# Decoder layer: self attention's sums passed inside the chip, products by pairs of key blocks, feed-forward weights made in cross attention

## The reference

```python
x = x + self_attention(layernorm(x))     # causal; scores (q W_cross) k mixed with a shifted k by a gate
x = x + cross_attention(layernorm(x))    # 77 context tokens, a mask
x = x + ffn(layernorm(x))                # silu(x Wg) * (x Wu), then Wd; the weights are int32 / 127
# attention, per head:
attn = softmax(scores); out = attn @ v; y = concat(out) @ Wo
```

## Time and profile before

| | us |
|---|---|
| median of 3 runs (1131.58 to 1135.62) | 1133.68 |
| the profiled execution | 1134.03 |
| its span, first to last instruction | 1132.3 |
| TensorE busy | 1044.6 (92%) |
| VectorE busy | 748.3 (66%) |
| ScalarE busy | 571.1 (50%) |
| GpSimd busy | 224.3 (20%) |
| bytes moved | 113.66 MB, mean 100 GB/s |

### The profile page before, as it was taken

The page is one execution under the profiler, slowest core; times in us unless marked ns, Lnnn a source line. Parts: engine busy times, 40 slices in busy tenths (PEclk is TensorE's granted clock), DMA queues, the critical chain, the costliest instruction groups (busy, mean ns, idle before and its releaser), DMA issues. The chain is left out here.

```text
span 1132.3 us, 19037 instructions
## 1 busy us (share of the span) xinstructions
PE 1044.6 (92%) x7092; PEld 608.6 (54%) x7092; DVE 748.3 (66%) x1603; ACT 571.1 (50%) x1043; POOL 224.3 (20%) x191
## 2 busy tenths in 40 slices
PE   2888989999999999999999895689989899999997
PEld 2777434444444444444444463344444688888886
DVE  5999887777887887877786374356544555555552
ACT  1445147667776677677666664646646211111110
POOL 6545550000000000000000032600000133333331
PEclk9999779999999999999999996889989899999998
DMA  7259844333334444444020045848774211111101
GB/s 244 104 198 251 248 86 74 73 75 70 71 70 89 90 86 88 89 89 86 23 76 27 35 130 187 204 89 171 169 177 126 80 43 49 51 53 50 48 9 37
DMA packets 89811, 113.66 MB, mean 100 GB/s; under 512 B 13822, under 2 KB 74922, under 8 KB 88183
## 3 DMA queue, kind: packets, MB, share of 16 engines
q1 hardware_dynamic: 86071, 107.43, 38.3%
q10 hardware_dynamic: 3648, 5.02, 2.1%
HBM read 66.26 MB, written 45.45 MB: 99 GB/s over the span
## 5 line engine op out<-in xcount | busy, mean ns | idle before, releaser
L782 ACT ACTIVATE prob<-bank 128x512 f32<-128x512 f32 (+1 forms) x608 | 329.2, 575 | 180.2 <-PE bank L826 101.5
L734 DVE TENSOR_REDUCE pm<-bank 128x1 f32<-128x512 f32 (+3 forms) x608 | 364.3, 655 | 82.5 <-PE bank L810 62.0
L805 PE MATMUL bank<-stk,stq 96*128 96x512 bf16 (+3 forms) x768 | 226.6, 339 | 2.7 <-DVE pm L734 2.1
L822 PE MATMUL bank<-stq,stk 98*128 98x512 bf16 (+3 forms) x768 | 222.4, 328 | 0.9 <-ACT prob L782 0.8
L836 PE MATMUL bank<-prob,va 128*17 128x512 f32 (+3 forms) x1536 | 164.0, 500 | 0.0
L805 PEld LDWEIGHTS bank<-stk,stq 96*128 96x128 bf16 x768 | 70.1, 98 | 153.5 <-DVE pm L734 114.1
L1554 ACT ACTIVATE e_sg<-bank 128x512 f32<-128x512 f32 x48 | 28.7, 598 | 188.7 <-PE bank L135 188.7
L967 POOL TENSOR_TENSOR c_rstd<-c_ve,mhalf 128x4 f32<-128x4 f32 x8 | 8.1, 1010 | 521.3 <-DVE c_ve L128 521.3
L1311 ACT ACTIVATE xprob<-bank 80x512 f32<-80x512 f32 x128 | 72.3, 592 | 65.5 <-PE bank L1349 64.0
L822 PEld LDWEIGHTS bank<-stq,stk 98*128 98x128 bf16 x768 | 69.2, 98 | 56.7 <-issue 12.2
L810 PE MATMUL bank<-tri_q,identb 128*128 128x128 bf16 (+2 forms) x352 | 88.3, 251 | 0.0
(11 more groups left out here) (172 smaller groups left out, 1379.4 us busy)
## 6 DMA issues: line engine op xcount, KB each, us to landing
qk<-a_parts SPq DMA_DIRECT2D x32, 384.0 KB, 4.3
od<-u_out SPq DMA_DIRECT2D x16, 512.0 KB, 3.2
oin<-od SPq DMA_DIRECT2D x32, 256.0 KB
od<-xu SPq DMA_DIRECT2D x16, 512.0 KB, 3.9
xq<-c_parts SPq DMA_DIRECT2D x16, 384.0 KB, 2.9
xstq<-xq SPq DMA_DIRECT2D x32, 192.0 KB, 4.3
stq<-qk SPq DMA_DIRECT2D x28, 192.0 KB, 4.6
stk<-qk SPq DMA_DIRECT2D x14, 384.0 KB, 7.1
```

Of the source, the lines that this page charges most:

```text
L734: nc.vector.tensor_reduce(pm[:, k, h0:h0 + hb, r], src[:, 0:hb * w].rearrange("p (h w) -> p h w", h=hb), AX, ALU.max).then_inc(s_mxe, 1)
L782: nc.scalar.activation(prob[:, U % NPS, 0:hb * n], bank[STB[U % NSB]][:, 0:hb * n], ACT.Exp).then_inc(s_ex, 1)
L805: mm = nc.tensor.matmul(dst[:, h * w:(h + 1) * w], stq[i][0:R, half, h0 + h, r * P:(r + 1) * P], stk[i][0:R, h0 + h, k0:k0 + w], start=(h ...
L822: mm = nc.tensor.matmul(dst[:, h * n:(h + 1) * n], stk[i][0:RM, h0 + h, kt * P:(kt + 1) * P], stq[i][0:RM, half, h0 + h, q0:q0 + n], start ...
```

## The change

- The sums and the denominators of self attention go by DMA from `u_out` straight to on-chip tensors `oall` and `den`: eight DMAs a group in place of one store, and no loads of them later. `shares` waits for these DMAs; `quotients` works in place and waits for no load.
- Two sets of products are issued one after the other when the second one's scores are 3 units old; `NPS` is 16. Self attention has three sets of buffers in place of four.
- In the middle stage `load_later`, without the weights, and the last sequence's shares come first on SyncE, and the shares first on VectorE. The weights' making leaves the stage.
- The weights are loaded in groups 0, 1 and 6 of cross attention and made in twelve pieces of 384 columns: ScalarE's two instructions after unit 6's exponential in groups 1 to 12, GpSimd's one ahead of its other work there.

```diff
-        NPS, LAG, LATE = 12, 3, 3
+        joint_end = [sets[s - s % 2 + 1][3] for s in range(len(sets))]
+        NPS, LAG, LATE = 16, 3, 3
...
-            plan += [("p", s, -1) for s, x in enumerate(sets) if x[3] - 1 == NST + u - LAG]
-            plan += [("p", s, 0) for s, x in enumerate(sets) if x[3] - 1 == u - LAG]
+            plan += [("p", s, -1) for s in range(len(sets)) if joint_end[s] - 1 == NST + u - LAG]
+            plan += [("p", s, 0) for s in range(len(sets)) if joint_end[s] - 1 == u - LAG]
...
             def store(g):
+                b, i = g // GB, g % GB
                 sp.wait_ge(s_u, 2 * g + 2)
-                sp.dma_start(od[g:g + 1].rearrange("a h w r t -> (a h w r) t"), u_out[:, g % 2]).then_inc(us[g % 2], 16)
+                for h in range(HG):
+                    row = HD * (HG * (i % 2) + h)
+                    sp.dma_start(oall[row:row + HD, b, i // 2],
+                                 u_out[h * VW:h * VW + HD, g % 2]).then_inc(us[g % 2], 16)
+                    row = S // DT * (HG * i + h)
+                    sp.dma_start(den[row:row + S // DT, b],
+                                 u_out[h * VW + HD:h * VW + VC, g % 2]
+                                 .rearrange("a (c t) -> a c t", t=DT)).then_inc(us[g % 2], 16)
...
-                    if g + GB - 1 < G:
+                    if g + NB - 1 < G:
                         sp.wait_ge(s_pv, g * NST)
-                        load_self(sp, g + GB - 1)
+                        load_self(sp, g + NB - 1)
...
         def quotients(v, c, k):
-            v.wait_ge(ldo[c % 3], 32 * (c // 3 + 1))
+            b, u = c // 2, c % 2
             v.wait_ge(s_bc, KT * c + k + 1)
-            nc.vector.tensor_tensor(oin[:, c % 3, k], bank[EB if c < N_EARLY else BB[k]][:], oin[:, c % 3, k],
-                                    ALU.mult).then_inc(s_on, 1)
+            o = oall[:, b, k, u * CH:(u + 1) * CH]
+            nc.vector.tensor_tensor(o, bank[EB if c < N_EARLY else BB[k]][:], o, ALU.mult).then_inc(s_on, 1)
...
         def mid_sync(sp):
-            for w in range(2):
-                sp.wait_ge(us[w], 16 * (G // 2))
-            load_den(sp, B - 1)
-            load_outputs(sp, 3)
-            load_outputs(sp, 4)
+            load_later(sp)
+            store_shares(sp, B - 1)
+            load_shares(sp, B - 1)
             for c in range(NCH):
-                if c + 5 < NCH:
-                    load_outputs(sp, c + 5)
                 for n in range(KT):
                     store_queries(c, n)
-                if c == 0:
-                    store_shares(sp, B - 1)
-                    load_shares(sp, B - 1)
-                    load_later(sp)
-                if c == 4:
-                    load_last_weight(sp)
...
         def mid_vector(v):
+            shares(v, B - 1)
             for k in range(KT):
                 quotients(v, 3, k)
             sums2(v, 2)
             for c in range(NCH):
                 for n in range(KT):
                     split(c, n)
-                if c == 0:
-                    shares(v, B - 1)
...
+        def load_weight(sp, n):
+            if n == 2:
+                sp.wait_ge(s_fl, NPC)
+            src = (gate_t, up_t, down_t)[n]
+            sp.dma_start(iw[:, n % 2].rearrange("p (t n) -> p t n", n=src.shape[1]),
+                         src.rearrange("(t p) n -> p t n", p=P)).then_inc(s_iw[n], 16)
+
+        def ffn_weight_high(a, x):
+            n, j = x // NPC, x % NPC
+            a.wait_ge(s_iw[n], 16)
+            i = iw[:, n % 2, j * PW:(j + 1) * PW]
+            nc.scalar.activation(i.bitcast(F32), i, ACT.Identity, scale=WSCALE).then_inc(s_ff, 1)
+            a.wait_ge(s_ff, 2 * x + 1)
+            nc.scalar.activation(piece((wg, wu, wd)[n][:, 0], j), i.bitcast(F32), ACT.Identity).then_inc(s_ff, 1)
...
+                if g < 2:
+                    load_weight(sp, g)
+                if g == 6:
+                    load_weight(sp, 2)
...
         def cross_gpsimd(g):
+            for x in range(3 * NPC):
+                ffn_weight_low(g, x)
             for c in range(2):
                 quotients3(g, c)
...
+                    if u == NST2 - 2 and 1 <= g <= 3 * NPC:
+                        ffn_weight_high(a, g - 1)
```

More of the change, by code:

```diff
@@ L697, in self_sync @@
                 b = g // GB - 1
-                if b >= 0 and g % GB == 1:
-                    for w in range(2):
[L700 to L704, removed]
                 if b >= 0 and g % GB == 2:
@@ L772, in outputs @@
                                      ACT.Identity).then_inc(s_u, 1)
-            for i in range(2, GB):
+            for i in range(2, NB):
                 a.wait_ge(s_set, i + 1)
@@ L835, in products @@
                 for h in range(HG):
-                    mm = nc.tensor.matmul(bank[PVB[half]][h * VW:h * VW + VC, q0:512], va[g % GB][:, kt, :, h],
+                    mm = nc.tensor.matmul(bank[PVB[half]][h * VW:h * VW + VC, q0:512], va[g % NB][:, kt, :, h],
                                           prob[:, (g * NST + first + h // hb) % NPS, (h % hb) * n:(h % hb + 1) * n],
@@ L860, in self_tensor @@
                         maxima(g + ahead, which)
-            for s, x in enumerate(sets):
-                if x[3] - 1 > NST - 1 - LAG:
+            for s in range(len(sets)):
+                if joint_end[s] - 1 > NST - 1 - LAG:
                     products(G - 1, s)
-        ldo = sems("c_ldo", 3)
-        s_den = sem("c_den")
         s_rd = sem("c_rd")
@@ L890, in program @@
         N_EARLY = 3
[L892 to L896, removed]
-                             .rearrange("g h r t -> (g h) r t")).then_inc(ldo[c % 3], 16)
-        def load_den(sp, b):
-            sp.dma_start(den[:, b], od[b * GB:(b + 1) * GB, :, 1, 0]
-                         .rearrange("g h (c t) -> (g h) c t", t=DT)).then_inc(s_den, 16)
         def store_shares(sp, b):
@@ L911, in shares @@
         def shares(v, b):
-            v.wait_ge(s_den, 16 * (b + 1))
+            for w in range(2):
+                v.wait_ge(us[w], NOUT * 2 * (b + 1))
             need(v, s_rs, 16 * (b - 1))
@@ new lines, in piece @@
+        def piece(w, j):
+            return w.rearrange("p t n -> p (t n)")[:, j * PW:(j + 1) * PW]
+        def ffn_weight_high(a, x):
[5 more added lines that the diff above has]
+            nc.scalar.activation(piece((wg, wu, wd)[n][:, 0], j), i.bitcast(F32), ACT.Identity).then_inc(s_ff, 1)
@@ L1208, in masks, with ffn_weight_low @@
+        def ffn_weight_low(g, x):
+            n, j = x // NPC, x % NPC
+            w = (wg, wu, wd)[n]
+            g.wait_ge(s_ff, 2 * x + 2)
+            nc.gpsimd.tensor_tensor(piece(w[:, 1], j), iw[:, n % 2, j * PW:(j + 1) * PW].bitcast(F32),
+                                    piece(w[:, 0], j).bitcast(F32), ALU.subtract).then_inc(s_fl, 1)
         def masks(a):
@@ L1621, in program @@
         keep = root.enter_context(ExitStack())
-        oin = sb(keep, "oin", [P, 3, KT, CH])
+        oall = sb(keep, "oall", [P, B, KT, S])
         rd = sb(keep, "rd", [3 * H, B, S], BF16)
```

78 lines of the change are left out of this document (28 added, 50 removed).

## The result

| | before | after |
|---|---|---|
| median of 13 runs each, same chip, us | 1138.13 (1131.58 to 1142.18) | 1126.37 (1118.12 to 1130.35) |
| the profiled execution, us | 1134.03 | 1129.87 |
| its span, and mean granted clock | 1132.3, 0.961 | 1128.1, 0.951 |

The ratio is 0.9886 (95% interval 0.986 to 0.9911): 1.1% faster, some 12 us, where 33.5 were forecast. 1126.37 lies outside the range of 1091 to 1116. The medians and ranges of times further down include a few executions in a slower state of the chip, which the ratios leave out.

What follows compares the result with a forecast made beforehand. TensorE's own work was taken to bound self and cross attention, and transfers waiting in SyncE's queue the middle stage. 1134.03 - 9.9 (pairs) - 1.2 (start) - 23.4 (middle stage) + 1.0 (cross attention) = 1100.5 us; range 1091 to 1116.

Steps and rivals of the forecast that it cites:

- The start stays: Start of the middle stage: no change in time, though SyncE issues eight transfers (5.0 us) after the last copy.
- I take 0.05 a group and 0.4 for the first weight: Cross attention: weights' pieces and a late first weight add 1.0 us; bounds 0 and 10.5 if every piece delays TensorE.
- What follows moves along.: After the middle stage: later work simply starts earlier, with no term of its own.
- the clock one rival: Middle stage: the last three chunks' queries run at the lower clock level, 7.9 us more, total 1108; chance 0.10.
- Pairs: Self attention: two sets issued together save 0.59 us a group, 9.9 us in all; bounds nothing and 17.3.
- The 1.08 for the last group: Last group of self attention: it makes no maxima, so pairing its sets saves the full 1.08 us.
- Both pair rivals: Self attention: pairing saves all of its 1.08 us a group, total 1093, chance 0.14; or nothing, 1110.4, chance 0.13.
- Start of self attention: First maxima: one constant less to fill moves GpSimd's additions earlier, saving 1.2 us; bounds 0 and 1.2.
- Middle stage: From the fourth chunk's queries to cross attention's first maxima: 33.20 us, saving 23.4; bounds 13.8 and 25.
- GpSimd stops VectorE: Cross attention: GpSimd's pieces block VectorE's casts through the shared port, costing 10.5 us in place of 1.0, total 1110; chance 0.08.
- SyncE's queue: Middle stage: transfers crowd in this queue and the 13.8 us idle stretch stays, total 1114; chance 0.07.
- the slower case: Self attention: VectorE's silence in each pair of products reaches 1.5 us, a group 33.0 us, total 1151; chance 0.03.

Runs made afterwards that it cites:

- SyncE's order as it was: Changed kernel with the last shares and the later stage's loads issued after the first chunk's stores again in the middle stage: 1127.0 us, ratio 0.9889.
- short quotients: Changed kernel with each of GpSimd's cross attention quotients made in eight instructions of 128 columns, not one of 1,024: 1121.77 us, ratio 0.9803.
- transfers behind the boundary: Changed kernel with the last group's eight transfers issued after the boundary between self attention and the middle stage: 1115.61 us, ratio 0.9798.
- order of the quotients: Changed kernel with GpSimd's first quotients after the ninth of its twelve pieces, not after all of them: 1122.8 us, ratio 0.9863.
- all three: Changed kernel with the eight transfers after the boundary, first quotients after the ninth piece, and quotients in eight steps of 128 columns: 1108.93 us, ratio 0.9733.
- the two made from it: Kernel before with two weights' loads moved to the third chunk's stores, 1134.4 us; kernel before without the weights' loads and making, 1123.63 us.

## Why the prediction was wrong

The mechanisms forecast for the pairs in eleven of fifteen groups and for the middle stage were there. The sum failed at three steps, and the range with them.

- **"The start stays"**, a term of nothing. A mechanism that was missing altogether. I had the eight issues (5.0 us) and asked only when the shares would be ready. What else waits for the end of SyncE's part of self attention I didn't ask: TensorE and ScalarE do. 6.78 us of wait for 1.74, the clock falls, 8.1 us in all; moving the issues behind the boundary took them back, and 10 us of the total.
- **"I take 0.05 a group and 0.4 for the first weight": 1.0 us for cross attention.** It was 13.1. The bound of 10.5 had the right kind of cause for a part of it, with the wrong object. The pieces (1.00 us against the 0.88 worked out) do end ahead of the casts, and a group is 8.06 us as forecast where nothing is waited for. But moving twelve pieces ahead of "its other work" moved the two quotients, of which I had no row, from two places into one. That they stand behind the pieces could be read from the diff. 4.2 us are waits of this kind and for loads, which now share the stage with 2.4 MB of weights: for casts 4.0 in place of 1.3, for loads of queries 3.7 in place of 2.6. The other 8.9 are the next step.
- **"What follows moves along."** This passes for a term of zero, but 8.9 of the 13.1 us in cross attention, the 2.5 ahead of it (3.4 more work time for the same matmuls, 0.9 less waiting) and 2.8 of the 3.0 in the last group are TensorE's clock. I gave the clock one rival and one place, the middle stage, where it was wrong: there it stayed at its upper level. That it could fall in any stage with waits was not in the range.
- *Pairs*: forecast 0.59 us a group, measured 0.59 in plain groups (29.87); in the three groups with shares 0.1 and in the first, at a lower clock, nothing, so 6.8 in place of 8.9 over the fifteen. The 1.08 for the last group is a term that failed by itself: at full clock pairs take 31.5 us there against 31.2, with a wait of 1.40 us for an early quotient where single sets wait 0.84. Both pair rivals fall.
- *Start of self attention*: the wait shrank by 1.09 us (4.28 for 5.37), forecast 1.2, but the projections ended 1.2 later (131.1 to 132.3), which is a matter of the execution: in the other kernels with the change they end at 131.2 to 133.5.
- *Middle stage*: 24.1 for 23.4, with no wait of TensorE over 3 us. The two bounds held, and not by luck: the steps from the fourth chunk's queries on are 8.45, 7.76, 5.27 and 5.37 us, forecast 8.44, 7.76, 5.78 and 5.78. What I took to be one queue were two causes, 13.3 for the weights and 10.8 for the rest, the sums above all; with no weights at all 8.3 of the 13.8 us of the long wait stay.
- *GpSimd stops VectorE*, chance 0.08: it happened in cross attention, by the quotients and not the pieces, but not at the price given. It made one wait of 4.00 us (1.26 before) and the 6.8 us at the lower clock behind it, some 6 us more than before. That the stage as a whole missed by 12.1, near this rival's 9.5, is luck. The Trainium skill ("SBUF — State Buffer", the section on SBUF's two separate sides) says that the port pair is held for the whole instruction and the loser fully blocks. The trace agrees: 2.19 and 2.26 us beside quotients of 2.3, 0.30 and 0.38 beside parts of 0.42.
- *SyncE's queue* and the slower case, VectorE's silences, did not occur.

Taken together the misses are 1.3 + 2.1 + 4.1 + 8.1 - 0.7 + 2.5 + 12.1 = 29.5 us, the distance from 1100.5 to 1129.87. (The terms are rounded; 29.37 is the exact distance.) Every rival priced one mishap alone; three came together, and the range did not allow for it.

**Left open**: why the clock falls in one execution of a kernel and not in another. In cross attention the first stretch at the lower level lasts 17 us in three profiled executions with all the pieces (changed, SyncE's order as it was, short quotients) and 3.4 to 6.8 in three others with them (transfers behind the boundary, order of the quotients, all three); without the pieces it is 3.4 and 6.8. Waits alone don't decide it. Short quotients waited less than the changed kernel and got a lower clock; the last kernel has waits of 7.9 us in the same stage at 0.99. All kernels with the change, and the three without it that were profiled (before, and the two made from it), run at a lowered clock at the first maxima of cross attention.

## What to carry to other kernels

When a change cuts one DMA into many, count the issues at the end of every block too: here TensorE and ScalarE stood there for the queue, and the clock fell behind the wait. When work goes ahead of an engine's queue, list what stands behind it and where that now falls, and keep GpSimd's instructions short where VectorE has small steps on the path. Quote a gain at one clock level (span times mean clock) and do not book what the clock gives in one stage: here the mean over all runs stayed at 0.956 though the middle stage rose from 0.85 to 1.00.

## What the runs showed of the hardware

- An issue of a small transfer from one on-chip buffer to another occupies SyncE for 0.52 us (16 rows of 4 KB) and 0.67 (the denominators', 4 KB in all), and eight of them 5.05 us; ScalarE and TensorE stood at the block's end until they were issued.
- The transfer of a two-row constant takes SyncE 5.5 to 6.2 us to issue, wherever in the queue it stood (5.96 before, 5.94 after, 5.53 to 6.15 in the other kernels), with or without weights beside it.
- GpSimd's elementwise step on float32 takes 0.42 us for 128 columns, 1.00 for 384 and 2.3 for 1,024. Beside it VectorE's reductions from the banks keep their 0.46 to 0.49 us, while casts and subtractions of 0.17 us from one on-chip buffer to another took up to 2.3 beside a step of 2.3.
- Runs of one kernel differ by up to 16 us with the mean granted clock: 1108.29 us at 0.970, 1124.77 at 0.949.
